# Layer two's residual is transposed by VectorE into one of two tiles, in place of TensorE and ScalarE through PSUM

## The reference

```
x = x + L0(x)                          # low-rank, per-batch coefficients
x = x + L1(x)                          # rmsnorm, attention (16 heads of 16), + SwiGLU of 1024
x = x + L2(x):
    qkv = x @ Wqkv.T + bqkv            # 16 heads, 256 tokens
    c   = tanh(x @ Wc1[:, :256].T + ...) @ Wc2.T   # "coherence" of a token and head
    attention scaled by a function of c, plus a field term, then @ Wout.T + bout
x = x + L3(x)                          # masked attention, rmsnorm, conditional scale and shift
```

## Time and profile before

| | us |
|---|---|
| median of 3 runs (1524.33 to 1525.01) | 1524.66 |
| the profiled execution | 1527.45 |
| its span | 1525.7 |
| TensorE busy | 1433.8 |
| VectorE busy | 1095.5 |
| ScalarE busy | 755.4 |
| GpSimd busy | 375.7 |

### The profile page before, as it was taken

The page is one execution under the profiler, slowest core; times in us unless marked ns, Lnnn a source line. Parts: engine busy times, 40 slices in busy tenths (PEclk is TensorE's granted clock), DMA queues, the critical chain, the costliest instruction groups (busy, mean ns, idle before and its releaser), DMA issues.

```text
span 1525.7 us, 29540 instructions
## 1 busy us (share of the span) xinstructions
PE 1433.8 (94%) x10155; PEld 1193.0 (78%) x10187; DVE 1095.5 (72%) x3672; ACT 755.4 (50%) x1667; POOL 375.7 (25%) x418
## 2 busy tenths in 40 slices
PE   2669999999999999999999999999999999999996
PEld 1457888888888888888877887887887787777774
DVE  7747666666666666665656778778778889888884
ACT  1336333434444444433334555655555666666674
POOL 7401000000000000000112332332323445454453
PEclk9879999999999999999999999999999999999997
DMA  7056233322223332232223345345355345445440
GB/s 283 1 77 87 40 50 50 50 43 50 43 38 50 50 50 49 34 61 36 43 43 78 66 64 86 64 65 85 59 72 85 73 78 97 81 75 96 80 77 15
DMA packets 101134, 100.02 MB, mean 66 GB/s; under 512 B 11494, under 2 KB 97640, under 8 KB 100346
## 3 DMA queue, kind: packets, MB, share of 16 engines
q1 hardware_dynamic: 100986, 98.14, 37.0%
HBM read 16.83 MB, written 4.19 MB: 14 GB/s over the span
## 4 chain that ended last, share of the span: by engine, by line
PE 78%; DVE 13%; issue 5%; ACT 3%; POOL 1%; DMA 1%; SPq 0%; DVEq 0%; ACTq 0%; POOLq 0%
PE bank L1271 15%; PE bank L1209 11%; PE bank L1220 10%; PE bank L1234 10%; PE bank L1130 9%; PE bank L1279 7%; PE bank L1258 5%; PE bank L1138 5%; PE bank L1146 2%; DVE c1t L553 2%; DVE rowmax L556 1%; DVE qk_lo L538 1%; DVE ot_raw L443 1%; DVE work L442 1%; PE bank L1218 1%
## 5 line engine op out<-in xcount | busy, mean ns | idle before, releaser
L1013 ACT ACTIVATE work<-bank 128x512 f32<-128x512 f32 x656 | 381.6, 598 | 189.4 <-PE bank L1220 141.1
L556 DVE TENSOR_REDUCE rowmax<-bank 128x2 f32<-128x512 f32 x512 | 335.6, 677 | 120.4 <-PE bank L1209 120.4
L1220 PE MATMUL bank<-qs,ks 98*128 98x256 f32 x1536 | 398.3, 342 | 2.5 <-DMA qs<-nm 1.1
L1209 PE MATMUL bank<-ks,qs 96*128 96x256 f32 x1536 | 339.0, 303 | 21.3 <-DVE qk_lo L538 9.8
L1220 PEld LDWEIGHTS bank<-qs,ks 98*128 98x128 f32 x1536 | 270.4, 192 | 49.8 <-issue 19.1
L1209 PEld LDWEIGHTS bank<-ks,qs 96*128 96x128 f32 x1536 | 245.1, 191 | 45.3 <-DVE qk_lo L538 13.1
L553 DVE CUSTOM_DVE_ANT_0 c1t<-bank,big_q 128x256 bf16<-128x256 f32 x512 | 192.3, 420 | 0.8
L1234 PE MATMUL bank<-work,vp 128*32 128x256 f32 x2816 | 174.7, 387 | 2.0 <-ACT work L1039 1.2
L1049 ACT ACTIVATE work<-bank 128x256 f32<-128x256 f32 x128 | 49.0, 383 | 256.4 <-PE bank L1271 256.4
L611 DVE SCALAR_TENSOR_TENSOR work<-work,bank 128x256 f32<-128x256 f32 x128 | 53.3, 417 | 114.5 <-ACT work L1049 114.0
L1279 PE MATMUL bank<-w_down,work 128*128 128x256 f32 x512 | 133.1, 382 | 0.0
(11 more groups left out here) (229 smaller groups left out, 2059.8 us busy)
## 6 DMA issues: line engine op xcount, KB each, us to landing
qs<-qk_hi SPq DMA_DIRECT2D x192, 128.0 KB, 3.9
ks<-qk_hi SPq DMA_DIRECT2D x192, 128.0 KB, 3.8
qs<-qk_lo SPq DMA_DIRECT2D x96, 128.0 KB, 4.3
ks<-qk_lo SPq DMA_DIRECT2D x96, 128.0 KB, 4.2
xres<-in_x_t SPq DMA_DIRECT2D x4, 1024.0 KB, 8.9
x_in<-in_x SPq DMA_DIRECT2D x16, 256.0 KB, 2.7
out<-xres SPq DMA_DIRECT2D x15, 256.0 KB, 3.8
qs<-nm SPq DMA_DIRECT2D x96, 16.0 KB
```

Source lines behind the costliest of these rows:

```text
L556: a = dve.tensor_reduce(rowmax[:, :, k:k + 1], bank[:, :].rearrange("p (t s) -> p t s", t=TC), AX, ALU.max)
L1013: act.activation(tile, scores, ACT.Exp, scale=HD ** -0.5).then_inc(L.probs.sem, 1)
L1209: m = pe.matmul(bank[:, t * S:(t + 1) * S], qs[par][0:SCORE_ROWS, k, t * P:(t + 1) * P], ks[par][0:SCORE_ROWS, k, :], start=True, stop=True)
L1220: m = pe.matmul(bank[:, c * S:(c + 1) * S], ks[par][0:SHIFTED_ROWS, k, c * P:(c + 1) * P], qs[par][0:SHIFTED_ROWS, k, :], start=not lowere ...
```

## The change

In layer two `xT` is dropped on TensorE and ScalarE, and its bank use with it. A new step `xturn`, in four parts, is issued by VectorE. Part k takes the 32 partitions from 32k of `xres`, and transposes them as 32x32 blocks in four instructions, one for each 32 partitions of the result; each covers 32 partitions and 128 elements. Parts 1 and 3 each count the event that q, k, v and coh1 wait for. The result goes to `yt` in even batches from 4 on, and to `xt` in the others. So from batch 4 on a batch is turned while the tile of the one before is still being read. Batches 0 to 3, in whose time the feed-forward part of layer one still uses `yt`, have all `xt` and are turned later, when v and coh1 of the batch before have been done. In their new slots the parts come in the order 0, 2, 1, 3 (batches 4 and up) and 0, 1, 2, 3 (the first four). Some slots of layers one and three and of layer two's q are moved by small amounts too.

```diff
+TURNS, LATE_TURN = 4, (-26.9, 0.5)
...
     1: {
...
-        "max": (-6.29, 2.84), "xT": -26.99, "q": -24.35, "stack": (-25.3, -22.08, -15.97, -16.88), "k": -22.83, "v": -12.2,
-        "load": -46, "rank": -32.95, "cond": -30.74, "squares": -28.24, "xn": -28.27, "oT": 18.5, "wo": 21.54, "yn": 23.31,
-        "yT": 24.38, "ffn": (25.73, 1.11), "down": (27.4, 1.24)},
+        "max": (-6.29, 2.84), "xT": -26.69, "q": -24.35, "stack": (-25.3, -22.08, -15.97, -16.88), "k": -22.83, "v": -12.2,
+        "load": -46, "rank": -32.95, "cond": -30.74, "squares": -29.5, "xn": -28.27, "oT": 18.5, "wo": 21.54, "yn": 23.31,
+        "yT": 24.38, "ffn": (25.73, 1.11), "down": (27.4, 1.21)},
     2: {
...
-        "max": (-6.52, 2.71), "xT": -26.47, "q": -24.49, "stack": (-23.72, -22.05, -15.9, -15.63), "k": -22.73, "v": -11.32,
+        "max": (-6.52, 2.71), "xT": -26.47, "q": -24.19, "stack": (-23.72, -22.05, -15.9, -15.63), "k": -22.73, "v": -11.32,
...
-        "wo": 22.05},
+        "wo": 22.05, "xturn": (-29.47, -28.24, -28.47, -27.97)},
     3: {
...
-        "max": (-6.13, 2.38), "xT": -26.55, "q": -23.59, "stack": (-24.46, -19.29, -15.9, -15.03), "k": -21.32, "v": -12.83,
-        "cap": -0.18, "expo": 2.6, "mod": 14.15, "oT": 16.94, "wo": 20.71, "squares": 22.54, "resid": 23.94},
+        "max": (-6.13, 2.38), "xT": -26.55, "q": -23.59, "stack": (-24.46, -19.29, -15.9, -15.03), "k": -20.99, "v": -12.83,
+        "cap": -0.18, "expo": 2.12, "mod": 13.06, "oT": 16.94, "wo": 20.71, "squares": 22.54, "resid": 23.94},
...
+def late_turns(steps):
+
+    return [(LATE_TURN[0] + LATE_TURN[1] * k if what == "xturn" else slot, what, k) for slot, what, k in steps]
...
-            steps += [(at + slot + LATER.get(engine, {}).get(what, 0), n, what, k, b) for slot, what, k in plan(n)]
+            steps += [(at + slot + LATER.get(engine, {}).get(what, 0), n, what, k, b)
+                      for slot, what, k in (plan(n) if n != 2 or b >= TURNS else late_turns(plan(n)))]
...
+                if what == "xT" and self.n == 2:
+                    return []
...
+        def turned_x(n, b):
+
+            return yt if n == 2 and b >= TURNS and b % 2 == 0 else xt
...
+                    if what == "xturn":
+                        if k == 0:
+                            dve.wait_ge(lay[1].x_new.sem, lay[1].x_new.at(b, 1))
+                            if b == 0:
+                                head.wait_filled(dve, 1, NBATCH - 1, "v")
+                            elif b == TURNS:
+                                head.wait_filled(dve, 1, NBATCH - 1, f"ffn{FC - 1}")
+                            else:
+                                was = b - (1 if b < TURNS else 2)
+                                head.wait_filled(dve, n, was, "v")
+                                head.wait_filled(dve, n, was, "coh1")
+                        to = turned_x(n, b)
+                        for q in range(QUADS):
+                            a = dve.transpose(to[HW * q:HW * (q + 1), :, :].rearrange("p c (t w r) -> p t w c r", t=TC, r=HW)[:, :, k, :, :],
+                                              xres[HW * k:HW * (k + 1), b, :, :].rearrange("p t (c q d) -> p t q c d", c=DC, d=HW)[:, :, q, :, :])
+                        if k % DC:
+                            a.then_inc(L.xt.sem, 1)
...
-                    if what == "xT":
+                    if what == "xT" and n != 2:
                         bank = head.wait_filled(act, n, b, "xT")
...
-                    if what == "xT":
+                    if what == "xT" and n != 2:
                         if n == 1:
...
-                        outputs_first(bank, w[:, "qk".index(what)], xt).then_inc(head.sem, 1)
+                        outputs_first(bank, w[:, "qk".index(what)], turned_x(n, b)).then_inc(head.sem, 1)
```

More of the change, by code:

```diff
@@ L57 @@
+        "cap": -0.18, "expo": 2.12, "mod": 13.06, "oT": 16.94, "wo": 20.71, "squares": 22.54, "resid": 23.94},
 }
-LATER = {"vector": {"q": -0.2, "k": 0.5, "ffn": 0.3, "oT": 0.5, "field": -0.34, "pv": 0.6, "coh2": 0.46, "squares": 0.41, "rz": 0.8, "norm": 1.2, "v": -0.29, "xn": 0.11, "stack": 1.16, "xT": -0.5}, "scalar": {"wo": 1.0, "pv": 0.2, "yn": -0.02, "oT": -0.25, "xn": -0.04, "ffn": -0.24, "xT": -0.33, "rz": -0.2, "k": 0.17}, "gpsimd": {"max": -0.28, "oT": -0.14, "q": -0.42, "xn": -0.41}, "sync": {"k": -0.01}}
+LATER = {"vector": {"q": -0.2, "k": 0.5, "ffn": 0.3, "oT": 0.5, "field": -0.34, "pv": 0.6, "coh2": 0.46, "squares": 0.41, "rz": 0.8, "norm": 1.2, "v": -0.29, "xn": 0.11, "stack": 1.16, "xT": -0.5}, "scalar": {"wo": 1.0, "pv": 0.2, "yn": -0.02, "oT": -0.25, "xn": -0.04, "ffn": -0.24, "xT": -0.33, "rz": -0.2, "k": 0.17}, "gpsimd": {"max": -0.28, "oT": -0.14, "q": -0.42, "xn": -0.5, "coh2": -0.02}, "sync": {"k": -0.01}}
@@ L1188, in step @@
                         bank = head.wait_free(pe, n, b, what)
-                        outputs_first(bank, w[:, "qk".index(what)], xt).then_inc(head.sem, 1)
+                        outputs_first(bank, w[:, "qk".index(what)], turned_x(n, b)).then_inc(head.sem, 1)
                     if what == "v":
                         bank = head.wait_free(pe, n, b, "v")
-                        tokens_first(bank, xt, w[:, 2]).then_inc(head.sem, 1)
+                        tokens_first(bank, turned_x(n, b), w[:, 2]).then_inc(head.sem, 1)
                     if what == "coh1":
                         bank = head.wait_free(pe, n, b, "coh1")
-                        outputs_first(bank, w_c1, xt).then_inc(head.sem, 1)
+                        outputs_first(bank, w_c1, turned_x(n, b)).then_inc(head.sem, 1)
                     if what == "coh2":
```

## The result

The changed kernel takes 1552.6 us (median of 4 runs, 1552.11 to 1554.91) against 1524.5 us: slower by a ratio of 1.0188 (95% interval 1.017 to 1.0206), +28.1 us. The kernel before is given here by the median of 4 runs. The forecast was +35.5 us, 1560, with 1527 to 1574 as its range.

A forecast was written before the change was run, and what follows sets the result against it. TensorE was taken as the bound, with VectorE's turns making it wait: 20.9 (steady batches) + 14.6 (first four) + 0 (layers one and three) = +35.5 us, on 1524.66 us, forecast 1560 us, range 1527 to 1574.

The forecast's parts named there:

- What bounds the kernel, and what is removed: TensorE bounds, busy 22.92 of 23.15 us in a steady layer-two batch; removing its transposes gives 7.0 us at most.
- One turn at 300 ns: One 32x128 transpose on VectorE, interpolated between 200 ns for 32x32 and 435 ns for 32x256.
- The spacing of 0.333: VectorE's turns start 0.333 us apart, each writing to another quarter; sixteen occupy 5.33 us; bounds 0.214 and 0.465 us.
- The steady batch: Layer two, batches 4 to 15: smax5 waits for smax3 behind the turns; period 24.90 instead of 23.16 us, +20.9 us.
- The first four: Layer two, batches 0 to 3: TensorE's q waits for the late turns on VectorE; together +14.6 us.
- Layers one and three: Moved slots: nearly nothing to gain in layer one; layer three's qk_lo waits give -9.6 to +9.6 us, taken as 0.
- Rival A: The turns on VectorE overlap, 0.214 us apart: +6.5 us, 1531 us; chance 0.18.
- rival C: Waits that the turns bring eat just the 7.0 us: within 0.2%, 1524.7 us, 1521 to 1528; chance 0.04.
- Rival B: TensorE stays the bound and all turns are hidden, needing turns under 0.197 us apart: -7.0, 1517.7 us; chance 0.09.

The follow-up runs named there:

- experiment 6: Changed kernel with four 128-partition transposes a batch in place of sixteen, the exchange between quarters left out: 1508.48 us against 1524.01 for the kernel before.
- experiment 5: Changed kernel with turns writing to the same 32 partitions they read, so blocks don't change partitions: 1526.3 us against 1524.01 for the kernel before.
- experiment 1: Kernel before with only layer three's three moved slots (k, expo, mod): 1517.24 us against 1524.43 for the kernel before, ratio 0.9944.
- experiment 3: Changed kernel with layer two's batches 0 to 3 transposed by TensorE and ScalarE as before: 1533.53 us against 1524.43 for the kernel before.

## Why the prediction was right

The direction, the place of the waits and their mechanism were right. That the number came near is in part luck: two terms were off by 5.6 and 5.8 us in opposite directions.

- What bounds the kernel, and what is removed: held. With the turns made cheap TensorE is the bound again, and each steady batch is 0.44 us shorter than before (experiment 6).
- One turn at 300 ns: measured 299 and 300. The spacing of 0.333 was a little high: (2.51 - 0.30)/7 = 0.316, and 0.297 in turn 0. The reason given for it, the change of quarter, was tested by experiment 5 for the quarter that is written, and held; a change of the quarter that is read was not tried apart. The Trainium skill's rule (VectorE: DVE Perf Modes, section Two Vector instructions with no wait between them) says that such an instruction is held until all earlier ones are done, and the trace agrees with 0.82 against 1.19 us for four. The 75 ns beside 1.04 ns a column of another page of the Trainium skill (Vector Engine (DVE) Microarchitecture Reference, section Measured stream behaviour on trn2), an estimated 0.21 us, are near the 0.19 us apart of experiment 5, (0.82 - 0.24)/3 with the last at 0.24, and not near these turns at 0.30 to 0.32.
- The steady batch: the loop rz, turns, smax3, smax5, q, qk_lo, rz was the right one. Its last leg was forecast at 12.78 and is 12.77 us, smax5 to qk_lo at 3.70 and is 3.62. The leg with the turns is 0.4 us shorter (rz at 929.51 by the period, smax5 at 937.55: 8.04 instead of 8.42), nearly all by the spacing. So +1.27 a batch, not +1.74: 15.3 us, where the term was 20.9. This is a size, not the mechanism.
- The first four: term 14.6, measured 20.4. The later starts were right: against the delay that its batch came with, q starts 3.9, 4.1, 4.1 and 2.75 us later than before; I had 4.50, 4.25, 4.25 and 2.90. What the term put at nothing is the clock behind the waits: q alone is 1.7 to 1.9 us longer four times, 7.2 us. Batch 2 gets its share back, since the 2.26 us for which TensorE waited for `yn` before are gone whole, where I had 1.3 us of them absorbed. The errors of the steady term (5.6 too high) and of this one (5.8 too low) nearly cancel by luck: 35.5 forecast for layer two, 35.7 measured.
- Layers one and three, taken as 0 with 9.6 either way: layer three gains 8.5 in this trace and 7.2 alone (experiment 1). My reason, that VectorE's own order decides when qk_lo is read, was wrong: TensorE's waits for it went (8.7 us from 1160 to 1500 us before, 0.7 in experiment 1). This term is most of what lies between 1560 and the measured 1553; layer one's +1.5 is in the noise of the start.
- Rival A (overlap) needed turns 0.21 apart. Experiment 5 has them, and at 1526 us with layer three's gain inside it is near what A gives (1531 less 7); with that gain it is rival C's case, 1521 to 1528. Rival B wanted turns under 0.197 us apart and the late ones hidden; experiment 6, with four transposes in place of sixteen, comes nearest: 1508.5, where B with 7 us of layer three's gives 1511, and the late ones are not quite hidden (3.6 us of waits).

## What to carry to other kernels

When an engine has as much idle time as an addition takes, the addition still costs wherever something waits for what stands behind it: walk the order once around the loop with real durations, and mark the resource whose next-but-n user waits. Idle time counts only if the work can be placed in it, and here 5.0 us of turns in 5.2 us of idle time made a steady batch 1.28 us longer, and 0.6 us even in the better order that was tried. Where a wait can't be avoided, count the clock behind it too: here it was 7 us on top of 16. And when slots are moved along with a change, time them alone: here they were the only gain.

## What the runs showed of the hardware

- A 32-partition transpose of VectorE that writes to another quarter than the last one costs about 0.1 us more than one that doesn't: four take 1.19 us instead of 0.82 and eight 2.51 instead of 1.78, at the same shape (experiment 5).
- A transpose of 128 partitions and 128 columns takes no longer than one of 32 partitions (281 against 300 ns), as this group of experiment 6's kernel shows:
```profile
L549 DVE STREAM_TRANSPOSE xt<-xres 128x128 f32<-128x128 f32 x40 | 10.5, 281 | 3.0 <-issue 1.7 <-PE bank L1168 1.1 <-PE bank L1239 0.2
```
- Each of the four idle stretches of 3.0 to 4.7 us on TensorE was followed by a granted clock of 0.50 to 0.57 over the next 4 us; behind 16.4 us of such waits q alone took 7.2 us longer. The waits of 0.9 us in the steady batches left the clock at 1.00. But a wait needn't be that long: in the trace of the kernel before, waits of 0.89, 0.21 and 0.18 us at 822 to 825 us were followed by this window at 0.50, and the 2.26 us for `yn` left the clock up there and were followed by 0.65 over 4 us in experiment 3.
```profile
827.00:831.00 4.00, 4.00 (x34) 2.19 (x36) 2.63 (x9) 1.22 (x3) 0.00 (x0) 0.50 0.66 108
```
